# Row-maximum products of an attention kernel: 64 contraction rows in place of 128

## The reference

```python
x = x + 0.5 * ffn(layernorm(x), Wg, Wu, Wd, Wr, temperature)     # 8 experts, gated
x = x + attn(layernorm(x), ...)
x = x + 0.5 * ffn(layernorm(x), Wg, Wu, Wd, Wr, temperature)

# attn, 16 heads of 64:
c_q, c_kv = h @ w_down_q.T, h @ w_down_kv.T
q, k, v = (up-projections of c_q, c_kv), split into heads
q, k = rope(q), rope(k)
scores = einsum('bhqd,bhkd->bhqk', q, k) / 8
attn = softmax(scores, axis=-1)
out = einsum('bhqk,bhkd->bhqd', attn, v)  ->  @ w_out.T + residual
```

## Time and profile before

| | |
|---|---|
| median of 3 runs | 1619.16 us (1617.44 to 1619.26) |
| the profiled execution | 1617.76 us, of which the span of the profile is 1616.0 us |
| TensorE busy, in the span | 1544.8 us (96%) |
| VectorE busy | 1388.6 us (86%) |
| GpSimd busy | 1302.6 us (81%) |
| ScalarE busy | 1227.6 us (76%) |
| mean granted TensorE clock | 0.987 of full speed |
| row-maximum products, line 892 | 1024 of them |

### The profile page before, as it was taken

How to read it: one execution, slowest core, us unless ns; L and a number is a source line. 1 busy time by engine, 2 the same in 40 slices (tenths; PEclk the granted TensorE clock), 3 DMA queues, 4 the chain that set the end, 5 groups by cost and what they waited for, 6 DMA issues and landing times.

```text
span 1616.0 us, 47776 instructions
## 1 busy us (share of the span) xinstructions
PE 1544.8 (96%) x19008; PEld 1023.5 (63%) x19008; DVE 1388.6 (86%) x2856; ACT 1227.6 (76%) x1711; POOL 1302.6 (81%) x912
## 2 busy tenths in 40 slices
PE   3999868999999999999999999999999999989999
PEld 2677634666666666666666666666666666656776
DVE  4546778999999999999999999999999998966443
ACT  3344367888888888888888888888888888884442
POOL 1555455999999999999999999999999997764555
PEclk9999989999999999999999999999999999999999
DMA  6333221112121211112121212111121212003444
GB/s 173 115 117 114 71 55 25 45 47 51 32 51 32 64 47 42 41 42 48 44 51 31 51 33 68 43 41 42 41 54 39 51 32 51 22 2 100 125 125 125
DMA packets 65627, 96.15 MB, mean 60 GB/s; under 512 B 11776, under 2 KB 24064, under 8 KB 65152
## 3 DMA queue, kind: packets, MB, share of 16 engines
q1 hardware_dynamic: 62320, 92.18, 21.6%
q10 hardware_dynamic: 3088, 0.92, 0.3%
HBM read 40.24 MB, written 2.36 MB: 26 GB/s over the span
## 4 chain that ended last, share of the span: by engine, by line
PE 78%; DVE 3%; ACT 2%; POOL 2%; issue 2%; DMA 1%; POOLq 0%; SPq 0%; DVEq 0%
PE ps L918 14%; PE ps L892 13%; PE ps L919 13%; PE ps L938 8%; PE ps L940 8%; PE ps L936 7%; PE ps L907 3%; PE ps L479 2%; PE ps L900 2%; PE ps L886 2%; PE ps L885 2%; POOL area L586 1%; DVE area L1051 1%; PE ps L463 1%; PE ps L464 1%
## 5 line engine op out<-in xcount | busy, mean ns | idle before, releaser
L1256 POOL TENSOR_TENSOR area<-area 128x1024 f16<-128x1024 f32 (+1 forms) x512 | 833.2, 1646 | 89.0 <-ACT area L1176 79.4
L1051 DVE TENSOR_REDUCE area<-ps 128x1 f32<-128x512 f32 x1024 | 664.5, 683 | 10.2 <-PE ps L892 7.6
L1174 ACT ACTIVATE area<-ps 128x1024 f16<-128x1024 f32 x512 | 525.1, 1026 | 141.6 <-PE ps L919 141.4
L938 PE MATMUL ps<-cv_all,area 128*128 128x64 f16 x4096 | 457.4, 195 | 0.0
L936 PE MATMUL ps<-cv_all,area 128*128 128x65 f16 x4096 | 455.6, 193 | 0.6 <-POOL area L1256 0.5
L940 PE MATMUL ps<-cv_all,area 128*128 128x65 f16 x4096 | 454.4, 193 | 0.0
L938 PEld LDWEIGHTS ps<-cv_all,area 128*128 128x128 f16 x4096 | 381.9, 97 | 78.9 <-issue 0.3
L936 PEld LDWEIGHTS ps<-cv_all,area 128*128 128x128 f16 x4096 | 384.5, 97 | 59.8 <-issue 9.0
L892 PE MATMUL ps<-area 128*128 128x512 f16 x1024 | 388.8, 380 | 5.6 <-DVE area L1051 5.4
L918 PE MATMUL ps<-area 128*128 128x512 f16 x1024 | 389.1, 380 | 2.3 <-ACT area L1176 0.6
L919 PE MATMUL ps<-area 128*128 128x512 f16 x1024 | 389.5, 380 | 0.0
(11 more groups left out here) (176 smaller groups left out, 2138.5 us busy)
## 6 DMA issues: line engine op xcount, KB each, us to landing
area<-area SPq DMA_DIRECT2D x384, 128.0 KB, 2.7
area<-f_w_rows_in_dram SPq DMA_DIRECT2D x128, 256.0 KB, 3.3
xg<-in_x SPq DMA_DIRECT2D x4, 512.0 KB, 7.8
out_x<-xg SPq DMA_DIRECT2D x3, 512.0 KB, 4.5
area<-in_wup SPq DMA_DIRECT2D x1, 1024.0 KB, 8.1
cs<-in_rope SPq DMA_DIRECT2D x1, 1024.0 KB, 8.9
area<-area SPq DMA_DIRECT2D x64, 2.0 KB
area<-in_wo ACTq DMA_DIRECT2D x1, 512.0 KB, 7.5
```

The lines of the kernel that those rows point to most:

```text
L938: nc.tensor.matmul(o[:, 0:DH], p_hi[:, s % 4, c:c + P], latents[:, DH + 1:CV], start=False, stop=False, skip_group_check=True)
L1051: nc.vector.tensor_reduce(mx[:, hd, kh, qt:qt + 1], bank, AX.X, ALU.max).then_inc(s_mr, 1)
L1174: nc.scalar.activation(p_hi[:, s % 4, :], sc, ACT.Exp, scale=0.125).then_inc(s_e16, 1)
L1256: nc.gpsimd.tensor_tensor(p_lo[:, s % 4, c0:], src[:, (s // 2) % 2, :], p_hi[:, s % 4, c0:], ALU.subtract).then_inc(s_pp, 1)
```

## The change

The row-maximum product reads only rows 0 to 63 of both operands. It now multiplies the queries' high halves with the keys' high halves; before, the low halves of the queries were in the sum too. Its output has the same shape and bank, and the number, order and waits of all instructions are the same on all engines. Nothing else is touched: the stacking transfers, the score products and the maximum over the 512 columns stay.

```diff
                         qt, kh = i // 2, i % 2
-                        last = nc.tensor.matmul(bank, qk["Q1"][:, slot, hd, P * qt:P * qt + P],
-                                                qk["K1"][:, slot, hd, 512 * kh:512 * kh + 512], start=True, stop=True)
+                        last = nc.tensor.matmul(bank, qk["Q1"][0:64, slot, hd, P * qt:P * qt + P],
+                                                qk["K1"][0:64, slot, hd, 512 * kh:512 * kh + 512], start=True, stop=True)
```

## The result

The changed kernel is slower. Its median is 1817.66 us (4 runs, 1815.76 to 1818.65) against 1618.3 us (4 runs, 1617.22 to 1619.26). The ratio is 1.123, with a 95% interval of 1.121 to 1.125. That is 199 us more, where 140 were forecast, and it lies above the range of 1612 to 1790 us. The mechanism was the forecast one, and its price was wrong.

A forecast was written before the change was run, and what follows sets the result against it. TensorE was taken to bound the kernel. Matmul and load at 0 us plus 1996 changes of shape x 0.07 = 140 us on 1617.8 gave 1758 us (chance 0.42), range 1612 to 1790 us.

The forecast's parts named there:

- The bound: In steady attention, 300 to 1300 us, TensorE is busy 998.95 of 1000 us, so the kernel pays its row-maximum products' cost.
- Matmul and load themselves at 0: Row-maximum product: halving the rows changes neither its streaming of 512 columns nor its 128-column weight load, 0 us each.
- The two changes of shape for each run: Each run of row-maximum products is entered from the full array and left for it: 998 x 2 = 1996 changes.
- nothing: Rival: no change of shape costs anything, the next load is taken beside the running matmul; 1618 us, chance 0.28.
- a long matmul covers the wait: Rival: 512-column products hide the wait, only the 466 entries behind line 940 pay; say 1650 us, chance 0.12.
- only the entry: Rival: entering the 64-row shape costs 0.07 us, leaving it is free; 1688 us, chance 0.10.
- The full tail: Rival: each change of shape pays a matmul's whole modelled tail, 0.164 us; 1945 us, chance 0.05.
- The price: Each change of shape at a row-maximum run adds 0.07 us (0.045 + 0.025), read from line 201's late load.
- The wait, taken as 0.045 us: At each change of shape, between end of streaming and next load: 0.09 us at half clock, 0.045 if scaled.
- The load in the open: At each change of shape the weight load is no longer hidden; the matmul starts behind it, taken as 0.025 us.
- TensorE has no slack: In steady attention, 300 to 1300 us, matmuls stand in a full queue, so the kernel pays any row-maximum product's cost.
- The unscaled wait: If the wait at each change of shape does not scale with the clock: 0.115 us a change, 230 us, 1848 us.

The follow-up runs named there:

- the control: Every row-maximum product done twice in a row into the same bank, both over 128 rows, against the kernel before: 1824.71 us.
- the probe of its kind: Kernel before with a transpose of 8 float32 columns of a constant weight ahead of each row-maximum product: 1717.8 us.
- each probe: Kernel before plus an overwritten 64-column product ahead of each row-maximum product; weights 64 x 128: 1844.54, 128 x 64: 1861.91, 128 x 32: 1847.31, 128 x 128: 1642.83 us.

## Why the prediction was wrong

**The bound** was right. What TensorE pays for these products, the kernel pays, and it ended 198 us longer.

**Matmul and load themselves at 0** were right: the second of two 64-row products in a row adds the plain 0.216 us. The reading for it was weaker than it looked, though. The 427 ns of line 430 are those of a transpose and the 417 ns of line 201 those of an ordinary product, both modelled.

**The two changes of shape for each run** were right in kind, number and place: entry and exit both pay, behind 65 columns as behind 512. With that the rivals "nothing" (0.28), "a long matmul covers the wait" (0.12) and "only the entry" (0.10) fell. The full tail (0.164 us for each change) fell as well. A unit has 32 runs, not the 31.5 of the last paragraph, which changes little: 4.5 us forecast, 6.49 measured.

**The price was the step that failed**: 0.07 us taken, 0.10 measured. Both terms of it were off.

- *The wait, taken as 0.045 us because it "scales with the clock".* It does not halve with it. At the full clock the load of line 892 starts 0.120 us behind line 940, in the median, and 0.307 behind line 919. With 0.029 and 0.216 us of streaming taken off, the wait is 0.091 us both times, twice what I took. The changed kernel has three such products in a stretch at the lower of the two clock levels (1.2 GHz in place of 2.4), and below line 918 and an entry come first, then an exit:

```profile
267.27 0.63 PE L918 MATMUL ps<-area 128*128 128x512 f16 x1
267.70 0.63 PE L919 MATMUL ps<-area 128*128 128x512 f16 x1
268.26 0.61 PE L892 MATMUL ps<-area 64*128 64x512 f16 x1
...
264.20 0.60 PE L892 MATMUL ps<-area 64*128 64x512 f16 x1 [1.97 <-DVE area L1051]
264.74 0.61 PE L918 MATMUL ps<-area 128*128 128x512 f16 x1
```

  512 columns stream there in 0.43 us, from line 918 to line 919. The entry takes 0.567 us by the unrounded starts, 0.14 more, and the exit 0.54, 0.11 more. The kernel with each product twice over 64 rows has the same at this clock: 0.567 us into the tile, and 0.560 out of it behind the second product, 0.13 more. But the product that stands first behind a change is followed 0.03 us sooner than a plain one (0.40 us and not 0.43), where at the full clock it is 0.01 later. With that taken in, an entry and an exit together cost 0.22 us at half the clock and 0.21 at the full one. A cost that scales would have been 0.42 at half the clock. These are a handful of events in each trace. "The emptying of an array is a count of its cycles" was an argument, not a reading, and it decided for 140 us in place of 230.

- *The load in the open, taken as 0.025 us more.* The load starts 0.01 us or less before its matmul (804.73 and 804.74). Over the whole stretch it is 0.004 us, so this term was next to nothing. The 0.09 us read at line 201 were nearly the whole price; with them alone the sum would have been 1996 x 0.09 = 180 us. That this number fits so well is partly luck: line 892 shows 0.14 us at an entry at the same half clock, and why line 201 showed less is open.

What is above 0.09 is the late follower: each first product behind a change, in the tile or behind it, is 0.226 us ahead of the next and not 0.216.

**"TensorE has no slack"** was nearly right. The kernel before has one stall in each unit, behind a product of line 892 that itself waits on three semaphores (stacked queries, stacked keys, the bank), with line 918 waiting on two more. What holds it there the profile does not name ("issue"). Timeline of PE, and the waits from 300 to 1300 us:

```profile
1055.63 0.39 PE L892 MATMUL ps<-area 128*128 128x512 f16 x1
1056.06 0.38 PE L918 MATMUL ps<-area 128*128 128x512 f16 x1
...
PEld ps L918 <- issue: 8.3, 27, 0.3
```

It takes 0.43 us in place of 0.22, some 0.2 us x 31 = 6 us in all. In the changed kernel 0.02 us a unit are left of it, and in the kernel with each product twice over 128 rows nothing. So a little added time on TensorE was free, which I had missed. The full 0.208 us for a run make 6.7 us a unit, and less the 0.2 of this stall they make the 6.49 measured. In the control the stall accounts for more than half of the 12 us left open above, and the last three units before the final one, which grew by 6.3, 5.4 and 5.4 us in place of 6.7, for 3 more.

**The range** failed by a choice of mine. The unscaled wait was in the text, at 1848 us, and I cut it off at 1790, since I held "nothing" to be too likely to leave out. This 0.28 rested above all on line 452. Line 452 is a transpose, and the probe of its kind shows that such a one pays nothing for a change of tile. Without it, line 201 and its control would have been the only evidence. The control was clean, so a range of about 1750 to 1850 was what the rows supported.

**The page of the Trainium skill** "TensorEngine Tiling (Array Packing)", section "Tiling Modes", says that a change of tiling mode drains TensorE. The runs agree in that every change to a tile with fewer rows or fewer columns and back brings a wait, about 0.10 us each way. A float32 transpose of 8 columns costs nothing beyond its streaming, though the built program gives it a tile of 128 x 32; whether it changes the mode at all, no run shows.

## What to carry to other kernels

A product over 64 rows is not cheaper than one over 128, and if it stands alone among full-array products it costs 0.2 us more, about as much as 512 columns. Keep all products of a dense stretch on one tile, if need be with rows that the result doesn't need, or put the small-tile ones side by side where the order allows it at no cost. When a trace has one event of the kind that a change multiplies by two thousand, read its price as it stands and widen the range to the other readings of that event; a neighbouring event that contradicts it has first to be of the same kind.

## What the runs showed of the hardware

- To leave the tile of 128 x 128 for one of 64 x 128, 128 x 64 or 128 x 32 and to come back costs 0.20 to 0.21 us in all (0.197, 0.214 and 0.200 for each probe).
- The wait begins with the end of the previous product's streaming: about 0.10 us come on top behind 64 and 65 columns (0.13 and 0.12 us from start to start) as behind 512 (0.31 and 0.32). Both ways together cost 0.21 us at the full clock and 0.22 at half of it.
- No weight load starts early across a change: it came 0.004 us before its own matmul, where it had come up to 0.21 us before.
- Products over 96 rows do not pay this price: they cost 0.003 us more each. A transpose of 8 float32 columns is exempt, the same operands as an ordinary product are not (0.400 against 0.096 us for each, 0.11 of it for a second matmul).
